# A graph network kernel: the opening stage rebuilt (host layouts, float32 degree loop, fills on one queue)

## What is computed

```python
edge_index = jnp.stack([src, dst])
h = jnp.maximum(_layernorm(x, axis=-1), 0.0)
x = x + layer0(h, edge_index, edge_weight, edge_attr_64, ...)
h = jnp.maximum(_layernorm(x, axis=-1), 0.0)
x = x + layer1(h, edge_index, edge_weight, ...)
```

## Time and profile before

| | |
|---|---|
| Median of 3 runs | 1908.72 us (1906.43 to 1911.76) |
| Profiled execution: its own time, its span | 1886.7 us, 1885.1 us |
| Busy, share of the span: TensorE, VectorE, ScalarE, GpSimd | 86%, 76%, 63%, 65% |
| Mean granted TensorE clock | 0.931 |
| Moved by DMA | 398.56 MB, 211 GB/s over the span |
| Opening and first steps | to about 178 us |
| Layer 0's messages in rhythm | about 178 to 693 us |
| Layer 1's messages, then the nodes | to about 1080 us, to the end |

### The profile page before, as it was taken

One profiled execution on the slowest core, in us unless ns is written; L12 is line 12 of the kernel. 1 busy time (PEld: TensorE's weight loads), 2 busy tenths in 40 slices (PEclk: granted clock), 3 DMA queues, 4 the chain that ended last, 5 costly groups with the idle time before them and its releaser, 6 DMA issues.

```text
span 1885.1 us, 30557 instructions
## 1 busy us (share of the span) xinstructions
PE 1625.4 (86%) x6531; PEld 1087.2 (58%) x6531; DVE 1430.1 (76%) x5731; ACT 1185.6 (63%) x2297; POOL 1216.8 (65%) x849
## 2 busy tenths in 40 slices
PE   4927999999999985676675349999999999999999
PEld 2314666666666653454454126666666666666666
DVE  7955777777777747877776487888888888888873
ACT  4924666666666631222222268899998989899984
POOL 2032888878788736888887765666666666666660
PEclk9967999999999997878878669999999999999999
DMA  6996666666666664655556589999999999999981
GB/s 231 418 404 235 182 179 183 194 181 177 193 188 178 176 189 101 123 109 108 119 107 136 96 199 263 249 268 264 271 270 270 269 267 271 268 270 271 270 234 75
DMA packets 150749, 398.56 MB, mean 211 GB/s; under 512 B 21586, under 2 KB 60060, under 8 KB 150700
## 3 DMA queue, kind: packets, MB, share of 16 engines
q1 hardware_dynamic: 89388, 264.75, 41.7%
q0 software_dynamic: 56416, 115.46, 32.5%
q10 hardware_dynamic: 4896, 17.83, 2.4%
HBM read 217.73 MB, written 180.23 MB: 211 GB/s over the span
## 4 chain that ended last, share of the span: by engine, by line
PE 51%; POOL 23%; DMA 8%; DVE 7%; issue 6%; SPq 1%; ACTq 1%; ACT 1%; POOLq 0%; DVEq 0%
PE bank L1314 9%; POOL sums_dram L514 9%; PE bank L1427 8%; PE bank L1416 8%; POOL kept L588 5%; PE bank L1321 5%; DMA out_dram<-cg 4%; PE bank L1351 4%; PE bank L1307 4%; POOL b_rs L510 4%; POOL cg L518 4%; PE bank L1255 4%; DVE cg L984 3%; DMA sums_dram<-ub,sidx 2%; PE bank L1295 2%
## 5 line engine op out<-in xcount | busy, mean ns | idle before, releaser
L1416 PE MATMUL bank<-kept,w 128*128 128x512 f32 x784 | 356.4, 598 | 0.0
L1427 PE MATMUL bank<-w_sb,kept 128*128 128x256 f32 x1568 | 354.3, 379 | 0.0
L588 POOL TENSOR_TENSOR kept<-kept 128x1024 f32<-128x1024 f32 x98 | 232.2, 2370 | 180.5 <-DVE cg L984 180.5
L1427 PEld LDWEIGHTS bank<-w_sb,kept 128*128 128x128 f32 x1568 | 297.9, 190 | 81.9 <-issue 46.4
L514 POOL DMA_INDIRECT sums_dram<-ub,sidx x148 | 243.1, 1643 | 76.8 <-issue 43.0
L1380 PE MATMUL bank<-cg,en 128*128 128x256 f32 x386 | 131.7, 485 | 124.1 <-ACT cg L1153 62.2
L510 POOL TENSOR_TENSOR b_rs<-b_ve,minus_half 128x8 f32<-128x8 f32 x102 | 208.7, 2047 | 28.7 <-DVE b_ve L1001 28.7
L1416 PEld LDWEIGHTS bank<-kept,w 128*128 128x128 f32 x784 | 142.8, 192 | 143.1 <-issue 143.0
L1191 ACT ACTIVATE kept<-kept,b_nb,b_rs 128x256 f32<-128x256 f32 x392 | 202.3, 589 | 21.5 <-DVE b_nb L974 21.5
L1181 ACT ACTIVATE kept<-kept,b_nb,b_rs 128x256 f32<-128x256 f32 x392 | 202.3, 589 | 11.0 <-DVE b_nb L974 11.0
L1314 PE MATMUL bank<-qkv_w,zT 128*128 128x512 f32 x392 | 192.7, 614 | 19.0 <-ACT zT L1070 19.0
(11 more groups left out here) (200 smaller groups left out, 3362.2 us busy)
## 6 DMA issues: line engine op xcount, KB each, us to landing
sums_dram<-cg SPq DMA_DIRECT2D x162, 512.0 KB, 5.4
kept<-in_x_dram SPq DMA_DIRECT2D x97, 512.0 KB, 5.7
kept<-sums_dram POOLq DMA_DIRECT2D x97, 512.0 KB, 10.0
cg<-sums_dram SPq DMA_DIRECT2D x97, 512.0 KB, 8.6
out_dram<-cg SPq DMA_DIRECT2D x97, 512.0 KB, 9.8
sums_dram<-cg ACTq DMA_DIRECT2D x34, 512.0 KB, 8.5
row_d<-in_dst_dram SPq DMA_DIRECT2D x48, 128.0 KB, 3.6
row_k<-keys_dram SPq DMA_DIRECT2D x24, 256.0 KB, 4.6
```

Of the source, the lines that this page charges most:

```text
L588: pool.tensor_tensor(X1[k.slot(8)], X[k.slot(4)], H[k.slot(2)], ALU.add).then_inc(g_xh, 1)
L1416: ins = pe.matmul(bank[:, 2 + m, :], w01[:, c, m * P:(m + 1) * P], hT[k.slot(2)][:, c * GN:(c + 1) * GN], start=(c == 0), stop=(c == KC - 1))
L1427: ins = pe.matmul(to, rT[k.slot(2)][:, c * GN + j * P:c * GN + (j + 1) * P], w2_sb[:, c, :], start=False, stop=(c == KC - 1), skip_group_c ...
```

## The change

*Host layouts.* The inputs come in other shapes: `ends` (dst and src, padded to 98 chunks, interleaved for node_i), padded dst, src, attributes and weight (as columns), the four vectors in one array, Wq, Wk, Wv turned and side by side, Wo and W turned, Wdk and Wdv turned with their biases as the last row, and `bo` and `b2` repeated four times. All transposes, the copies out of them and the clears of padding go. The weight loads (9 instead of 18, with b2) are issued by ScalarE at the very start.

*Degree loop in float32.* One matmul a chunk, two VectorE operations, nothing on ScalarE. VectorE runs 80 chunks (HOT_LOOPS) straight, then 6 in each of the message steps 1 to 3. TensorE runs 48 (HOT_FIRST), then the folding matmuls, then the other 50, all ahead of its message steps.

*Fills.* All 98 by SyncE, straight after node_i, the weights of the edges, rows_b and dst. At fill 72 and 84 (LOADS_AT) stand the loads of pairs 2 and 3, each with its waits. Keys, spare rows and the zeros of sums1 come behind the fills.

*GpSimd* makes the constants in another order and does the index work (`edges`, 13 operations) between the gathers of pair 1 and pair 2. It starts to gather as soon as `ends` has landed.

*VectorE* spreads the rest over its steps: the subtractions in step 1, bias rows, folded weights and the cosine in step 2, degrees, cutoff and keys in step 3, inverse roots in step 5. ScalarE takes the cosine in step 3 and the root in step 4. TensorE's first product with Wo waits for the degrees, which now lie in its bank.

The diff, cut to its core:

```diff
 @block.sync
-            sp.wait_ge(s_zero, 1)
-            for i, t in enumerate((src, dst, edge_weight)):
...
-            for i in range(FILLS_FIRST):
-                sp.dma_start(group(sums0, Step(i)), rows_b).then_inc(s_fill, 16)
...
+            sp.dma_start(node_i[:, :, :], ends).then_inc(s_ends, 16)
+            sp.dma_start(ew_f[:, :], edge_weight).then_inc(s_ew, 16)
+            sp.dma_start(rows_b, bo.rearrange("(a d) -> a d", a=1).broadcast_to([P, G * D])).then_inc(s_fillrow, 16)
+            sp.dma_start(e_dst[:, :], dst.rearrange("(c p) -> c p", p=P)).then_inc(s_rows, 16)
...
-            run_steps(sp, EP, LATER, 2, 2, load_edges)
+            for k in range(2):
+                load_edges(Step(k))
+            sp.wait_ge(s_fillrow, 16)
+            for i in range(NG):
+                if i in (LOADS_AT, LOADS_AT + 12):
+                    load_edges(Step(2 + (i - LOADS_AT) // 12))
+                sp.dma_start(group(sums0, Step(i)), rows_b).then_inc(s_fill, 16)
+            sp.dma_start(sums0[ROWS:ROWS + P, :], rows_b[:, 0:D]).then_inc(s_fill, 16)
+            sp.wait_ge(s_key, 1)
+            sp.dma_start(keys.rearrange("(c p) -> c p", p=P), e_keyf[:, :]).then_inc(s_keys, 16)
+            sp.wait_ge(s_zero, 1)
+            for i in range(1, Q):
+                sp.dma_start(sums1[N + i * SPARE:N + i * SPARE + P, :], rows_0[:, 0:D]).then_inc(s_fill1, 16)
+            run_steps(sp, EP, LATER, 2, 2, load_edges, start=LATER)
 @block.gpsimd
+            def edges():
+                link(pool.tensor_copy(dump_f[:, :], dump_i[:, :]))
+                link(pool.tensor_scalar(part_f[:, :], dump_f[:, 0:1], float(-N), None, ALU.add))
+                link(pool.tensor_copy(dst_f[:, :], node_i[:, :, 0]))
+                link(pool.tensor_copy(src_f[:, :], node_i[:, :, 1]))
+                link(pool.tensor_scalar(valid[:, :], edge_no[:, :], float(E), None, ALU.is_lt))
+                for t, ends_f, of in ((off_d, dst_f, 2), (off_s, src_f, Q)):
+                    for i in range(of):
+                        link(pool.tensor_scalar(t[:, i:EC:of], ends_f[:, i:EC:of], dump_f[:, i:i + 1], None,
+                                               ALU.subtract))
+                    link(pool.tensor_tensor(t[:, :], t[:, :], valid[:, :], ALU.mult))
+                pool.sem_inc(s_edges)
-            pool.wait_ge(m_ib, 1)
+            pool.wait_ge(s_ends, 16)
             for p in range(EP + MESSAGE_STEPS):
+                if p == 2:
+                    edges()
                 messages(p)
 @block.vector
+                dve.tensor_scalar(hot_p[q][:, :], iota_p[:, :], col(pkey, k), col(ew_f, k), ALU.is_equal, ALU.mult)
+                dve.tensor_scalar(hot_c[q][:, :], iota_c[:, :], col(ckey, k, 1), None, ALU.is_equal).then_inc(s_hot, 1)
...
+                if s.reg is None and 1 <= s.off <= 3:
+                    at0 = HOT_LOOPS + HOT_STEP * (s.off - 1)
+                    for k in range(at0, min(at0 + HOT_STEP, EC)):
+                        hot(Step(k))
+                        j = k - at0
+                        if s.off == 1 and j < 4:
+                            subtract_first(j // 2, j % 2)
+                        if s.off == 2 and j < 2:
+                            bias_row(j)
+                        if s.off == 2 and j == 3:
+                            folded()
+                if s.reg is None and s.off == 2:
+                    cosine()
+                if s.reg is None and s.off == 3:
+                    dve.memset(fill_0, 0.0).then_inc(s_zero, 1)
+                    degrees()
+                    dve.wait_ge(s_edges, 1)
+                    cut_off()
...
+                if s.reg is None and s.off == 5:
+                    inverse_roots()
 @block.scalar
+            act.dma_start(vectors[:, :, :], columns).then_inc(s_qkv, 16)
+            act.dma_start(wq_t[:, :, :], qkv_t.rearrange("(c p) k -> p c k", p=P)).then_inc(s_qkv, 16)
...
+            act.wait_ge(s_qkv, 32)
+            for k in range(KC):
+                ins = act.activation(qkv_w[:, k, :], wq_t[:, k, :], ACT.Copy, scale=g_col[:, k:k + 1])
+            ins.then_inc(s_turned, 1)
             def messages(s):
-                if s.reg is None and s.off >= 2:
-                    at0 = FILLS_FIRST + FILLS_STEP * (s.off - 2)
-                    for i in range(at0, min(at0 + FILLS_STEP, NG)):
-                        act.wait_ge(m_nm1, s.off - 1)
-                        act.dma_start(group(sums0, Step(i)), rows_b).then_inc(s_fill, 16)
+                if s.reg is None and s.off == 3:
+                    act.wait_ge(s_cos, 1)
+                    act.wait_ge(s_dve, 1)
+                    act.activation(cut[:, :], cut[:, :], ACT.Sin, bias=half_pi[:, 0:1], scale=-1.0).then_inc(s_cos, 1)
+                if s.reg is None and s.off == 4:
+                    act.wait_ge(s_deg, 1)
+                    act.activation(root[:, :], deg1[:, :], ACT.Sqrt).then_inc(s_rsq, 1)
 @block.tensor
-                for i in range(3):
-                    pe.wait_ge(*((s_hot, k.value(1, 2)) if i == 0 else (s_hotw, k.value(1))))
-                    ins = pe.matmul(bank[:, 2, 0:COLS], hot_p[q][:, 1 + i, :], hot_c[q][:, :],
-                                    start=first and i == 0, stop=last and i == 2)
+                pe.matmul(bank[:, 6, 0:COLS], hot_p[q][:, :], hot_c[q][:, :], start=first, stop=last).then_inc(s_hotmm, 1)
+            for k in range(4):
+                hot(Step(k))
+            with pe.Fori(1, HOT_FIRST // 4) as reg:
+                for u in range(4):
+                    hot(Step(u, reg, 4))
+            pe.wait_ge(s_ldw, 96)
...
+            with pe.Fori(HOT_FIRST // 4, HOT_LOOPS // 4) as reg:
+                for u in range(4):
+                    hot(Step(u, reg, 4))
+            for k in range(HOT_LOOPS, EC):
+                hot(Step(k))
```

More of the change, by code:

```diff
@@ L28 @@
 AHEAD = 5
-FILLS_FIRST = 64
-FILLS_STEP = 8
+HOT_FIRST, HOT_LOOPS = 48, 80
+HOT_STEP = 6
+LOADS_AT = 72
 CUTOFF = 5.0
@@ L90, in run_steps, with build @@
         body(Step(s))
-def build(nc, x, src, dst, edge_attr, edge_weight, ln_g, ln_b, Wq, bq, Wk, bk, Wv, bv, Wo, bo,
-          Wdk, bdk, Wdv, bdv, W, b, W1, b1, W2, b2, out):
+def build(nc, x, ends, dst, src, edge_attr, edge_weight, columns, qkv_t, qkv_b, wo_in, wd_in, w_in, w1_in, w2_in,
+          bo, b2, out):
     ctx = ExitStack()
@@ L162, in build @@
         w2_sb = sb("w2_sb", [P, KC, D])
[L163 to L166, removed]
+        vectors = sb("vectors", [P, 4, KC])
+        g_col, b_col, b0_col, b1_col = [vectors[:, i, :] for i in range(4)]
         b01_col = sb("b01_col", [P, KC])
@@ L406, in load_edges @@
                 if k.within(EP):
-                    wide = E - (EP - 1) * 2 * P if k.reg is None and k.off == EP - 1 else 2 * P
                     if k.past(2):
                         pass_on(sp, (m_D, k.value(-1, 2)))
-                    sp.dma_start(aT[q][0:R, 0:wide], edge_attr[:, bass.ds(k.value(0, 2 * P), wide)]
+                    sp.dma_start(aT[q][0:R, :], edge_attr[:, bass.ds(k.value(0, 2 * P), 2 * P)]
                                  ).then_inc(m_attr[q], 16)
@@ L696, in hot, with col @@
-            def hot(s):
-                k = s
+            dve.wait_ge(s_ew, 16)
+            def col(t, k, *i):
+                return t[(slice(None), bass.ds(k.value(0), 1), *i)]
+            def hot(k):
                 q = k.slot(4)
@@ new lines, in bias_row, with folded @@
+            def bias_row(i):
+                w = (0, 512)[i]
+                wide = min(512, 3 * D - w)
+                link(dve.tensor_tensor(qkv_w[0:1, 0, w:w + wide], rows[:, w:w + wide], bank[0:1, 4 + i, 0:wide],
+                                       ALU.add))
+            def folded():
+                dve.wait_ge(s_pre_pe, 2)
+                link(dve.tensor_copy(w01[:, :, :].rearrange("p k d -> p (k d)"), bank[:, 3, :]))
+                dve.tensor_tensor(b01_col[:, :], b1_col, bank[:, 2, 0:KC], ALU.add).then_inc(s_ready, 1)
@@ L749, in messages @@
             def messages(s):
-                if s.reg is None and s.off == 2:
-                    weights()
                 a, g, z, m = s.back(1), s.back(2), s.back(3), s.back(4)
@@ L1446 @@
     arrays, args = {}, []
-    for name in _INS:
-        a = np.ascontiguousarray(inputs[name].T if name == 'edge_attr_64' else inputs[name])
+    for name, a in laid_out(inputs).items():
+        a = np.ascontiguousarray(a)
         arrays[f"in_{name}_dram"] = a
```

342 lines of the change are left out of this document (125 added, 217 removed).

## The result

The changed kernel took 1872.1 us (median of 4 runs, 1868.97 to 1874.83) against 1907.9 us for the kernel before on the same chip (4 runs, 1906.43 to 1911.76): a ratio of 0.982, 95% interval 0.9805 to 0.9837, 35.8 us less. The forecast was 1866 us, 43 us less. The profiled execution has a span of 1867.3 us.

The account below looks back on a forecast made before the run. The opening, before TensorE's full-clock rhythm of 10.92 us a pair, was taken to bound the gain: loop, pairs and fills put the first scatter at 150 instead of 193.8, so 43 us off the 1908.72 median gives 1866 us, range 1852 to 1888.

Parts of the forecast that it names:

- Start of the loop: Degree loop: the first matmul stands at about 6 us instead of 31.27, with 4 us taken for the first load.
- A chunk: Degree loop: 0.66 us a chunk, bound by TensorE, with VectorE's two operations at 0.60 against 0.69 before.
- the 0.37 row: Earlier profile row: 392 float32 columns in SBUF take VectorE 0.37 us, against 0.57 from PSUM; basis for 0.60 a chunk.
- the rival of one column a cycle: Degree loop: VectorE writes float32 at the slower rate, 0.87 us a chunk; gain 27, 1882 us; chance 0.12.
- Half clock: Degree loop: 3 us added for TensorE running at half clock at the loop's start.
- Pairs 0 and 1: First message pairs: 12 + 14 = 26 us against 32.6, with pair 0 still at half clock; pair 2 at 131.
- The fills: SyncE's queue: it waits for pair 0 until about 113 us, so the fills end at 150 and release the first scatter.
- First scatter: GpSimd, message stage: released by the fills at about 150 us instead of 193.80, 43 us earlier.
- Then 10.9 us a pair: Message stage: after the first scatter the rhythm stays at 10.9 us a pair, so the earlier start is kept.
- The rival at half clock: Degree loop: TensorE stays at half clock, 1.31 us a chunk; first scatter 18 us later, 1927 us; chance 0.04.
- Index work on GpSimd: Opening: GpSimd's 13 index operations run while it is otherwise idle and cost nothing, if VectorE is not held.
- GpSimd blocks VectorE: Rival, opening: GpSimd's operations and gathers hold VectorE, shifting everything by 12 us; gain 31, 1878 us; chance 0.08.

Follow-up runs that it names:

- experiment 5: Changed kernel with 34 of the fills back on ScalarE, eight a step from step 2, and 64 on SyncE: 1862.0 us, ratio 0.987 to the kernel before.
- experiment 2: Changed kernel with the loads of pairs 2 and 3 on ScalarE's queue, or at fills 84 and 96: 1851.7 and 1854.3 us, against 1852.9 unchanged.
- experiment 4: Changed kernel with one more 128-column float32 matmul in each of 44 degree-loop chunks: 1855.5 us, ratio 0.983 to the kernel before.
- experiment 3: Changed kernel with eight more fills (4.2 MB, to a tensor nothing reads) ahead in SyncE's queue: 1858.6 us, ratio 0.986 to the kernel before.

## Why the prediction was right, and where it was not

The time (1872, forecast 1866, range 1852 to 1888) and the sign were right, and the gain of 42 to 43 us was 35.8, 36.5 and 40.4 on three chips. By its own steps:

- *Start of the loop*, 6 us: 6.95. *A chunk*, 0.66 bound by TensorE: right. VectorE's own pace is 0.60 as forecast (0.62 and 0.58 at the start), and it then keeps TensorE's. Its 392 columns to float32 take 0.42 us, near the 0.37 row and not 0.57; so the rival of one column a cycle is out. The rule of the Trainium skill's page VectorE: DVE Perf Modes (What auto-detection actually checks) gave the same chunk of 0.60, and the trace agrees. (That no row of before has a float32 result from 16-bit columns was not quite so: its line 885 makes one, with a second operand from the bank, in 0.62 us.) *Weights* 6.8: 6.75. *Half clock* 3: 3.2 in size, but not shown as clock: the first 12 passes take 6.05 us (6.95 to 13.00), 0.50 each against 0.33 later, while the granted clock reads 1.00 there. *80 chunks* at 69: 69.7. *Last chunk* 99 to 101: 100.5. The 8.5 us set against a quick first load was the least time of a 512 KB fill in the earlier trace rows and not of a small load; the load took 4.71.
- *Pair 0* at 105: 102.95. *Pairs 0 and 1*, 26 us: 18.9 (102.95 to 121.82). This term was mis-sized: without ScalarE's fill issues TensorE goes from the loop's last chunks (until 100.46) almost straight into pair 0 with its clock full (four matmuls take 1.98 us, not 3.78), and VectorE's roots (121.98 to 128.04) fall behind the two pairs: it is pair 2 that takes 14.1 us. With the fills back on ScalarE (experiment 5) pair 0 takes 3.78 again, and pairs 0 and 1 29.9 us (115.23 to 145.11).
- *The fills*, 150: 153.6, and this is the step that failed; its number nearly held by luck, since two errors cancelled. I had SyncE wait from 100 to 113 with queued work covering "until 100". In fact 72 fills are issued by 98 us but moved only some 11 us later; SyncE's wait ended at 107.1, and no gap opened (forecast: some 12 us of gap near 100). I charged 13 us for a stall that costs nothing, and left out the 15 us that the last fill needs from issue (137.7) to landing; without the 13 my sum gives 137, which is when it was issued. Experiments 2 and 4 show the first, experiment 3 that bytes set the end.
- *First scatter* 43 earlier: 40.2, and 38.0 in the pair of traces from one chip. It was released by a fill, as forecast, and with more room than I had: pair 2 stood at 121.8, not 131. What the argument left out is that pair 4's attributes stand in the same queue behind the fills and arrive at the same moment.
- *Then 10.9 us a pair*: 11.02 against 11.08 on one chip, and so right there; 11.42 on the first. "A rhythm other than 10.9" was named as a sign that I was wrong; it was a sign of the chip or the execution.
- *Later stages unchanged*: from the last scatter into the second sums to the end are 823 us before (1070.6 of 1893.8) and 824.6 after (1028.3 of 1852.8). Right.
- *The rival at half clock* was summed wrongly: 125 us, the 36 us from the loop's 80 chunks to pair 0 and 12 more give 173 for pair 0, not 167, and so about 1933 us, not 1927. Nothing else hangs on it.
- *Index work on GpSimd*, nothing, and *GpSimd blocks VectorE*, 12 us: while GpSimd gathers (11 to 16 us) VectorE does 7 chunks in 5 us, 0.71 each, while it does the index work (16 to 23) 12 in 7, beside nothing (24 to 40) 24 in 16, 0.67, which is TensorE's pace. At its own 0.60 a chunk VectorE needs all of the 7 us for 12 chunks, with GpSimd busy for 5.95 of them, and 4.2 of the 5 us, with GpSimd busy for 4.06. That leaves no room for a block by whole instructions, though a loss of up to about 0.1 us a chunk beside the gathers can't be told. So the rival is out:

```profile
11.00:16.00 5.00, 2.29 (x7) 1.00 1.05 395
16.00:23.00 7.00, 3.80 (x12) 1.00 1.03 417
24.00:40.00 16.00, 8.31 (x24) 1.00 1.03 419
```

The Trainium skill's page SBUF - State Buffer (Who interferes with whom) would have VectorE stand for whole GpSimd instructions here, 4.1 us busy in the first window. The rows show no such loss, and the measurement decides. The index work itself was not moved back, so its price is told from these rows alone.

What the change bought is that the fills start at 8.4 us instead of 24.1 and run without a pause, with the computing side ahead of them. How much of the earlier computing that needed is told in part: from pair 2 on it has some 10 us to spare (experiment 2), but pair 0, behind which SyncE waits, has only some 3, since of its 8.8 us of delay 5.8 reached the first scatter (experiment 4). Experiment 3 prices the start of the fills (10.0 us of bytes ahead of them, 10.6 us at the first scatter), experiment 5 the single queue (10.8). The host layouts, the float32 loop and GpSimd's index work were not undone one by one, so what each would cost alone is not shown.

## What to carry to other kernels

A queue whose issues are held back by full DMA engines can keep moving when its issuer waits (here for some 11 us): price such a wait only beyond what is queued, and price the end of the queue by its bytes. When a start waits for a bulk transfer, list everything that hangs on that transfer (the load behind it, the work behind the waiting instruction, the buffers it frees): here three things hung on the fills; taking away one or two left the pow of step 10 within 1 us of where it was (188.4 to 190.1 against 189.4), or made it later, and taking away all three brought it 8 us earlier. Then follow an earlier start to the next stage before you count it: here it was not seen there. And compare profiled executions only with their own chip's: the same kernel differed by 1% between chips.

## What the runs showed of the hardware

- With fills of 0.5 MB queued, about 11 us of work (some 4.6 MB at 418 GB/s) still flowed after SyncE stopped issuing: no dip in a wait of 9.0 us, 56 GB/s from 110 to 117 us in a wait from 99.5 to 115.9.
- A load of 64 KB behind them in the same queue (pair 4's attributes) took 8.7 us in the changed kernel's first execution and 10.9 in the two others from issue to landing; from ScalarE's queue, issued at 133.3 us under the same DMA load, pair 4's was there when TensorE came to it at 148.2.
- The same program's message step was 11.02, 11.01 and 11.42 us on three chips, while from the last scatter to the end it took 824.6, 823.5 and 823.6 us.
